# Unread matrix products ahead of the waits of eight TensorE stages in a four-layer graph kernel

## The reference

```
layer 0: A = exp(8 tanh((xq)(xk)^T / sqrt(128) / 8)) * adj;  A / rowsum(A) @ x @ v
layer 1: x_h = elu(x Wi + bi); e = sigmoid(tgt_i + src_j + be) * mask;
         recv = elu([e @ x_h, x_h * rowsum(e)] Wn + bn);  [recv, x_h] Wm + bm
layer 2: relu(sum_k T_k(L) x W_k + bias), T_k(L) = I, L, 2 L L - I, L the scaled Laplacian
layer 3: 5 gated steps: av = [adj h, adj h]; z, r, hv from av and h;
         h = (1 - z) h + z hv
```

## Time and profile before

| | |
|---|---|
| median of 3 runs | 2041.39 us (2039.12 to 2041.62) |
| profiled execution | 2039.13 us, span 2036.8 us |
| busy, of the span | PE 1856.7 us (91%), DVE 1472.1 (72%), ACT 1354.7 (67%), POOL 921.1 (45%) |
| chain that ended last | PE 65%, DVE 13%, issue 8%, POOL 7%, ACT 7% |
| mean granted TensorE clock | 0.962 of full |

### The profile page before, as it was taken

One profiled execution on the slowest core, in us unless ns is written; L12 is line 12 of the kernel. 1 busy time (PEld: TensorE's weight loads), 2 busy tenths in 40 slices (PEclk: granted clock), 3 DMA queues, 4 the chain that ended last, 5 costly groups with the idle time before them and its releaser, 6 DMA issues.

```text
span 2036.8 us, 27531 instructions
## 1 busy us (share of the span) xinstructions
PE 1856.7 (91%) x9307; PEld 1442.9 (71%) x9307; DVE 1472.1 (72%) x3054; ACT 1354.7 (67%) x2689; POOL 921.1 (45%) x1009
## 2 busy tenths in 40 slices
PE   3899998899998999889998899989999889989997
PEld 2776776777767777577775777757768677676775
DVE  6786688766687667866778667786667866678666
ACT  0766677576766767566775667756768666686666
POOL 2354445445364442634436344363444544345344
PEclk6999999999999999999999999999999999999998
DMA  2000001000010000100000000100001000000000
GB/s 69 22 1 0 1 1 42 1 1 1 7 37 1 1 1 12 32 1 0 1 24 21 1 1 1 43 1 1 1 2 42 0 1 1 2 22 1 0 1 22
DMA packets 13514, 21.32 MB, mean 10 GB/s; under 512 B 2720, under 2 KB 5024, under 8 KB 13216
## 3 DMA queue, kind: packets, MB, share of 16 engines
q1 hardware_dynamic: 10768, 18.68, 2.7%
q10 hardware_dynamic: 2576, 0.53, 0.1%
HBM read 10.82 MB, written 8.39 MB: 9 GB/s over the span
## 4 chain that ended last, share of the span: by engine, by line
PE 65%; DVE 13%; issue 8%; POOL 7%; ACT 7%; DMA 0%; DVEq 0%; SPq 0%; POOLq 0%; ACTq 0%
PE psA L1080 7%; PE psA L1050 7%; PE psA L1051 7%; PE psA L881 5%; PE psB L886 5%; PE psB L888 5%; PE psB L887 5%; PE psA L886 3%; PE psA L888 3%; PE psA L887 3%; PE psB L949 3%; PE psA L949 3%; DVE E L753 2%; ACT X L471 2%; PE psB L1074 2%
## 5 line engine op out<-in xcount | busy, mean ns | idle before, releaser
L430 POOL TENSOR_TENSOR S<-S,H 128x512 f32<-128x512 f32 x160 | 225.1, 1407 | 486.3 <-ACT S L573 486.3
L1050 PE MATMUL psA<-adjT_hi,nh_hi 128*128 128x512 f32 x640 | 275.0, 430 | 11.9 <-ACT H L559 11.6
L471 ACT ACTIVATE X<-X,shift,rstd 128x128 f32<-128x128 f32 x512 | 210.4, 501 | 90.2 <-POOL shift L401 89.2
L1051 PE MATMUL psA<-adjT_hi,nh_lo 128*128 128x512 f32 x640 | 259.8, 406 | 0.0
L425 POOL TENSOR_TENSOR xT_lo<-H,xT_hi 128x512 fp32r<-128x512 f32 x160 | 219.2, 1383 | 71.0 <-ACT xT_hi L581 38.1
L841 DVE SCALAR_TENSOR_TENSOR E<-E 128x512 f32<-128x512 f32 x160 | 181.7, 1135 | 63.3 <-ACT E L577 60.4
L836 DVE SCALAR_TENSOR_TENSOR E<-E,H 128x512 f32<-128x512 f32 x160 | 128.5, 803 | 115.1 <-ACT E L567 114.7
L679 DVE TENSOR_TENSOR gT_lo<-psA,gT_hi 128x512 fp32r<-128x512 f32 x160 | 108.8, 688 | 115.0 <-ACT gT_hi L563 101.1
L396 POOL TENSOR_TENSOR neg_mean<-zero_cols,mv 128x4 f32<-128x4 f32 x128 | 30.8, 240 | 356.1 <-DVE mv L696 355.8
L1080 PE MATMUL psA<-E,u5T 128*128 128x512 f32 x320 | 165.0, 597 | 13.7 <-DVE E L836 13.7
L571 ACT ACTIVATE E<-psB,z_bias 128x512 f32<-128x512 f32 x160 | 110.4, 690 | 81.3 <-PE psB L1074 79.8
(11 more groups left out here) (224 smaller groups left out, 5317.1 us busy)
## 6 DMA issues: line engine op xcount, KB each, us to landing
xin<-in_x SPq DMA_DIRECT2D x32, 256.0 KB, 3.0
out<-X SPq DMA_DIRECT2D x32, 256.0 KB, 2.0
E<-in_adj SPq DMA_DIRECT2D x1, 1024.0 KB, 5.7
E<-in_L_gnn_w_w SPq DMA_DIRECT2D x3, 128.0 KB, 7.2
E<-in_L_gnn_weight SPq DMA_DIRECT2D x1, 192.0 KB, 6.8
E<-in_L_gnn_u_w SPq DMA_DIRECT2D x2, 64.0 KB, 6.9
Wm_sb<-in_L_gnn_Wm ACTq DMA_DIRECT2D x1, 128.0 KB, 7.0
E<-in_L_gnn_q SPq DMA_DIRECT2D x1, 64.0 KB, 5.5
```

Source lines behind the costliest of these rows:

```text
L430: nc.gpsimd.tensor_tensor(kept[s], kept[s], H[s][:, :], ALU.mult).then_inc(pool_done[s], 1)
L471: last = nc.scalar.activation(X[s][:, t, :], X[s][:, t, :], ACT.Identity, scale=rstd[s][:, t:t + 1], bias=shift[s][:, t:t + 1])
L1050: nc.tensor.matmul(psA[s][:, :], hi, adjT_hi[:, m, :], start=(m == 0), stop=False)
L1051: last = nc.tensor.matmul(psA[s][:, :], lo, adjT_hi[:, m, :], start=False, stop=(exact and m == TILES - 1))
```

## The change

A table `WARM` names eight pairs of stage and slot. At the head of the PE part of such a stage, ahead of its waits, `keep_warm` issues a number of products of the same two tiles: stationary `adjT_hi[:, 0, 0:128]`, moving `adjT_hi[:, 0, :]` (512 columns), each with start and stop set, written to a bank of PSUM whose content isn't needed at that time. Nobody reads the result and no semaphore is touched. In each tuple stand the slot, the bank (0 psA, 1 psB), the slot that owns the bank and the number of products.

```
+WARM = {"x0": [(0, 1, 0, 5)], "xh": [(0, 1, 0, 7)], "gates": [(1, 0, 1, 3)], "sums1": [(0, 1, 0, 4)],
+        "cheb01": [(0, 1, 0, 7)], "x3": [(0, 0, 0, 14)], "m0": [(0, 1, 0, 5)], "rh4": [(2, 1, 0, 9)]}
...
+            def keep_warm(name, s):
+
+                for slot, bank, owner, count in WARM.get(name, ()):
+                    if slot == s:
+                        for _ in range(count):
+                            nc.tensor.matmul((psA, psB)[bank][owner][:, :], adjT_hi[:, 0, 0:P], adjT_hi[:, 0, :],
+                                             start=True, stop=True)
+
             def stage_x0(s, r):
+                keep_warm("x0", s)
                 pe.wait_ge(loaded[s], 16 * r + 16)
                 pe.wait_ge(residual[s], NORMS * r + 1)
...
             def stage_xh(s, r):
+                keep_warm("xh", s)
                 pe.wait_ge(xT_lo_ready[s], XTS * r + XT["x1"])
...
             def stage_gates(s, r):
+                keep_warm("gates", s)
...
             def stage_sums1(s, r):
+                keep_warm("sums1", s)
...
             def stage_cheb01(s, r):
+                keep_warm("cheb01", s)
...
             def stage_x3(s, r):
+                keep_warm("x3", s)
...
             def stage_m(s, r, k, exact):
+                keep_warm(f"m{k}", s)
...
             def stage_rh(s, r, k):
+                keep_warm(f"rh{k}", s)
```

More of the change, by code:

```diff
@@ L164 @@
 NORMS = 4
+WARM = {"x0": [(0, 1, 0, 5)], "xh": [(0, 1, 0, 7)], "gates": [(1, 0, 1, 3)], "sums1": [(0, 1, 0, 4)], "cheb01": [(0, 1, 0, 7)], "x3": [(0, 0, 0, 14)], "m0": [(0, 1, 0, 5)], "rh4": [(2, 1, 0, 9)]}
 def build(nc, x, adj, q, k, v, Wi, bi, We, be, Wn, bn, Wm, bm, cheb_w, cheb_b,
```

## The result

The changed kernel takes 2062.0 us (median of 4 runs, 2061.0 to 2064.3) against 2040.7 us for the kernel before (2039.1 to 2041.6): ratio 1.0107, 95% interval 1.0091 to 1.0123. It is 21 us slower, and the time lies above the range that was forecast (2029 to 2048). The profiled executions have spans of 2036.8 and 2062.0 us, 25.2 us apart.

What follows compares the result with a forecast made beforehand. PE was taken as the fullest engine, though DVE sets the pace in places, with some 120 us of rounds and tail at half clock. Terms -16.9 + 9.2 + 2.9 + 2.8 = -2.0 us on 2041.4 gave 2039, range 2029 to 2048.

Steps and rivals of the forecast that it cites:

- the five ahead of x0: Five products behind the loop's return, not covered by its gap: 1.16 us a round at full clock, 9.2 us together.
- x0, 9.2 us: Cost of the five products at x0: 8.1 us in seven rounds, plus half of 2.1 us in round 0.
- All seven fit: The products at the seven stages other than x0 fit in PE's waits at full clock and cost nothing.
- (a): x0 to xh: low clock costs 1.40 us a round, 7.8 to regain; falls after the return's gap take 2.9.
- (b): xh to cheb01: low clock costs 0.1 us, since DVE sets the pace; 0.6 us to regain in four rounds.
- (c): cheb01 to x3: low clock costs 0.47 us a round; 1.4 us to regain in three rounds.
- (d): x3 to rh4's release: 1.21 us a round, about 5.1 in four rounds; 2.0 more from ACT's work coming forward.
- new gap ahead of uh0: PE idle 1.8 us after m0, before uh0 of slot 0; clock falls there in 1 of 4 rounds, costing 2.8 us.
- Rival C: Slower: the loop's return alone lets the clock fall every round; 2044 to 2051 us, taken as 2048; chance 0.23.
- Rival D: The whole penalty returns: 60 us of the 120 at half clock, less 9.2, giving 1991 us; chance 0.07.

Runs made afterwards that it cites:

- after_pad16: The changed kernel with 16 narrow products added once in the setup, moving the loop's start in PE's program: 2038.1 us, ratio 1.0002.
- only_x0: The kernel before with only the five products at x0 added: 2042.7 us, ratio 1.0032.
- only_x3m0: The kernel before with only the 14 products at x3 and 5 at m0 added: 2029.3 us, ratio 0.9960.
- no_x0_pad16: The changed kernel without the five products at x0 and with 16 narrow products added in the setup: 2027.8 us, ratio 0.9945.
- after: The changed kernel itself, with the products at all eight places, against the kernel before: 2062.0 us, ratio 1.0107.
- pad54: The kernel before with 54 narrow products added once in the setup, moving the loop's start: 2057.9 us, ratio 1.0092.
- no_x0: The changed kernel without the five products at x0, the other 49 kept: 2046.0 us, ratio 1.0038.
- only_rh4: The kernel before with only the nine products at rh4 of slot 2 added: 2043.3 us, ratio 1.0030.

## Why the prediction was wrong

- **The term that was missing.** The prediction took the change at x0 as five products, 1.16 us a return, and didn't count what 108 more instructions ahead of the loop do to its start. This is the step "the five ahead of x0": shown in its place is a second stretch of 2.1 to 2.65 us in each of six returns and the low clock that it brings, 21 to 24 us by after_pad16 (by ratios and by medians). Nothing in the sum or in the range stood for it. It could be seen: the row marked "issue" was taken as a fixed cost of the return, without asking what the return waits for and whether that depends on the program's length.
- **The rest of the sum** can be judged on after_pad16, which is the change without that term. It was forecast at -2.0 us and a ratio of 0.999; measured is 1.0002 (0.9992 to 1.0011). That it came so close is in part luck: the terms hit less well than their sum, and their errors cancel.
- *x0, 9.2 us*: only_x0 measured 6.5 (4 to 9), since the five alone also hold the clock; on top of the other 49 they cost 11.6 (6 to 17). At the start x0's transposes moved from 38.8 to 40.8 us, near the 2.1 that was forecast, and some of it came back, as forecast: in round 0, x0 to xh took 43.7 us against 44.4 before, and 42.6 in only_x0 and in after_pad16.
- *"All seven fit"*: right for xh, gates, sums1, cheb01, x3 and m0. Wrong for rh4: the gap was read in round 2 and taken for all eight. In rounds 0 and 7 it isn't there, 2 x 2.1 us.
- *(a), 7.8 us less 2.9*: with the clock up, x0 to x0 of slot 3 takes 10.5 us and not 12.1, 1.6 us a round; that part was there (after_pad16: 10.78 in the mean). The single gap of the return let the clock fall in two of six rounds of after_pad16 and not in the others, near the 3 in 10 that were estimated (the forecast counted seven returns; there are six).
- *(b) and (c), 2.0 us*: 0.6 measured, -1.2 to 2.4. DVE's pace hides the clock there, as the earlier trace rows said.
- *(d), 5.1 + 2.0 - 2.8 = 4.3 us*: only_x3m0 measured 8.2 (5.5 to 11), 5.9 of it in this stretch by its profiled execution. The new gap ahead of uh0 came as forecast, but the clock didn't fall behind it, so the 2.8 were not to be subtracted. Its row in the changed kernel, forecast at 1.8 us:

```profile
665.30 0.50 PE L887 MATMUL psB<-xT_hi,U_hi 128*128 128x512 f32 x1 [1.70 <-POOL xT_lo L426]
```

- **Rival C** named the right place and the right effect, a low clock behind x0 in every round. The windows of the changed kernel from the first product at x0 to its transposes and from there to the next set's xh show it:

```profile
533.87:537.91 4.04, 1.93 (x5) 1.29 (x6) 0.00 (x0) 0.00 (x0) 0.00 (x0) 0.65 0.01 4
537.91:581.43 43.52, 43.37 (x284) 38.52 (x282) 31.57 (x103) 36.35 (x76) 15.99 (x31) 0.95 0.13 43
```

 The second takes 43.52 us at 0.95, the same as before: nothing of (a) came back. But C had this from the single stretch of the return, which after_pad16 refutes, and priced it at +9 at most. Rival D, the whole of the low-clock time returned, is refuted by the same run: its clock after 50 us is 1.00, and it gained nothing; without the five at x0 (no_x0_pad16, 1.00 up to the tail) it was 11 us. The Trainium skill's price of throttled time (TensorE: Matmul & The Clock Gate, "Terms") would return an estimated 60 us for the 120 at half clock; the runs show far less.

## What to carry to other kernels

An edit ahead of a hardware loop moves the loop's start in the instruction stream; before a small difference is put down to the edit, the same kernel should be timed with a few dozen idle-time instructions more ahead of the loop, since that alone was worth 0.9% here. A cover for added work has to be looked up in every kind of round, the first and the last too, and a stretch marked "issue" at a loop's return isn't a place to fill from behind: products ahead of the branch run for free at the returns, products behind it are paid. In this kernel of eight rounds, writing them out was worth more than warming the clock (1.9% against 0.5%).

## What the runs showed of the hardware

- A loop's return left PE idle for 0.3 to 2.6 us where no products stood ahead of the branch, and for a second stretch of 1.0 to 2.8 us when the loop's start stood close to the end of a 16 KB piece of program (after, pad54, no_x0). A piece's packet took 0.9 to 1.6 us. PE ran on 1.5 to 1.8 us after it had landed at a return, 1.2 to 1.7 us after it had landed at a second stretch.
- Products that stand ahead of the branch run during the fetch (eight in 2.01 us, then x0 after 0.14 us).
- Returns of other engines' loops show as ordinary waits on PE: 2.2 us at rh4, which stay when PE's loop alone is written out and go when those of DVE, ACT and POOL are too.
- The granted clock fell after two idle stretches next to each other (1.8 to 2.5 and 2.1 to 2.7 us) in every round of the changed kernel, after a single one of 2.23 and of 2.48 us in two of six rounds of after_pad16 and not after 1.74 to 2.08 us in the other four, nor after 1.7 us behind the products of m0. The length of a stretch alone doesn't decide it: in only_rh4 a return of 2.42 us was followed by a fall in round 3 and not in round 2, and in no_x0_pad16 the clock fell behind 2.08 us and stayed up behind 2.32.
